# Reordering neighbouring steps in the four hand-written engine orders of a decoder-layer kernel

## What is computed

```
S = S * exp(g_t);  kv = k_t S;  delta = (v_t - kv) * beta_t
S = S + k_t^T delta;  o_t = q_t S
```

## Time and profile before

| what | value |
|---|---|
| median of 3 runs | 2258.28 us (2253.6 to 2272.47) |
| the profiled execution's own time | 2256.81 us |
| its span, first to last instruction | 2255.0 us |
| mean granted TensorE clock | 0.972 of full speed |
| TensorE matmuls busy | 2098.6 us (93% of the span) |
| TensorE weight loads busy | 1805.4 us (80%) |
| VectorE busy | 1646.6 us (73%) |
| ScalarE busy | 1385.5 us (61%) |
| GpSimd busy | 803.3 us (36%) |
| the chain that ended last | TensorE 83%, VectorE 10%, issue 3% |
| instruction transfers (two queues) | 264 packets, 4.33 MB, and 107 packets, 0.88 MB |

### The profile page before, as it was taken

How to read it: one execution, slowest core, us unless ns; L and a number is a source line. 1 busy time by engine, 2 the same in 40 slices (tenths; PEclk the granted TensorE clock), 3 DMA queues, 4 the chain that set the end, 5 groups by cost and what they waited for, 6 DMA issues and landing times.

```text
span 2255.0 us, 81282 instructions
## 1 busy us (share of the span) xinstructions
PE 2098.6 (93%) x33098; PEld 1805.4 (80%) x33130; DVE 1646.6 (73%) x5291; ACT 1385.5 (61%) x4262; POOL 803.3 (36%) x1845
## 2 busy tenths in 40 slices
PE   4899999999999999999999999999999999999975
PEld 3788888888788888888888888888888888888864
DVE  4577777777777777777777777777777777777743
ACT  3576556776555776555677655677655677555642
POOL 3333334433234333334333333343334343324321
PEclk8899999999999999999999999999999999999987
DMA  6000000000000000000000000000000000000000
GB/s 227 7 2 8 10 10 9 10 4 7 10 10 10 10 5 9 8 10 10 9 5 10 8 10 10 9 10 4 8 10 10 9 10 4 7 10 10 7 4 5
DMA packets 25795, 30.66 MB, mean 14 GB/s; under 512 B 9264, under 2 KB 22592, under 8 KB 24656
## 3 DMA queue, kind: packets, MB, share of 16 engines
q1 hardware_dynamic: 25424, 25.46, 3.5%
HBM read 21.25 MB, written 4.19 MB: 11 GB/s over the span
## 4 chain that ended last, share of the span: by engine, by line
PE 83%; DVE 10%; issue 3%; SPq 2%; ACT 1%; POOL 0%; DMA 0%; DVEq 0%; POOLq 0%
PE bank_b L644 11%; PE bank_a L464 10%; PE bank_b L746 5%; PE bank_b L652 5%; PE bank_a L474 5%; PE bank_b L769 5%; PE bank_b L605 5%; PE bank_a L536 3%; PE bank_a L546 3%; PE bank_b L700 2%; PE bank_a L582 2%; PE bank_a L589 2%; PE bank_a L512 2%; DVE smax L1169 2%; PE bank_b L677 2%
## 5 line engine op out<-in xcount | busy, mean ns | idle before, releaser
L1021 DVE SCALAR_TENSOR_TENSOR acc<-ypad,convw,acc 128x128 f32<-128x128 f32 x1536 | 426.7, 346 | 109.4 <-ACT acc L823 109.4
L464 PE MATMUL bank_a<-xnT,wqkvz 128*128 128x128 f32 x2048 | 251.1, 279 | 27.2 <-DVE scoreT L1092 24.6
L464 PEld LDWEIGHTS bank_a<-xnT,wqkvz 128*128 128x128 f32 x2048 | 243.0, 195 | 36.6 <-issue 34.9
L1433 POOL TENSOR_SCALAR lnv<-mv 128x1 f32<-128x1 f32 x128 | 24.8, 193 | 582.9 <-DVE mv L1111 580.2
L934 ACT ACTIVATE prob<-bank_b,nmax 128x128 f32<-128x128 f32 x512 | 181.4, 382 | 6.7 <-DVE nmax L1171 4.2
L1387 POOL TENSOR_TENSOR ostat<-ostat 128x4 f32<-128x4 f32 x64 | 18.7, 293 | 456.3 <-ACT gseg L888 456.2
L914 ACT ACTIVATE prob<-bank_b 128x512 f32<-128x512 f32 x64 | 38.2, 597 | 211.7 <-PE bank_b L644 211.7
L1076 DVE TENSOR_TENSOR ablk<-bank_a,const 128x128 f32<-128x128 f32 x256 | 72.6, 284 | 105.7 <-PE bank_a L536 102.7
L823 ACT ACTIVATE acc<-bank_a,convw 128x128 f32<-128x128 f32 x512 | 147.9, 397 | 0.0
L644 PE MATMUL bank_b<-x2T,wg 128*128 128x128 f32 x1024 | 141.7, 296 | 0.0
L546 PE MATMUL bank_a<-ablk,xblk 32*32 32x32 f32 x8192 | 123.3, 195 | 15.6 <-DMA bk<-in_bk_dram 9.2
(11 more groups left out here) (252 smaller groups left out, 5626.0 us busy)
## 6 DMA issues: line engine op xcount, KB each, us to landing
xin<-in_x_dram SPq DMA_DIRECT2D x32, 128.0 KB, 2.4
cin<-in_ctx_dram SPq DMA_DIRECT2D x32, 128.0 KB, 2.8
out_dram<-yout SPq DMA_DIRECT2D x32, 128.0 KB, 1.7
wqkvz<-in_wqkvz_dram SPq DMA_DIRECT2D x6, 512.0 KB, 6.6
wout<-in_wout_dram SPq DMA_DIRECT2D x1, 1024.0 KB, 9.6
wg<-in_wg_dram SPq DMA_DIRECT2D x1, 1024.0 KB, 11.3
wu<-in_wu_dram SPq DMA_DIRECT2D x1, 1024.0 KB, 13.1
wd<-in_wd_dram SPq DMA_DIRECT2D x1, 1024.0 KB, 14.9
```

Source lines behind the costliest of these rows:

```text
L464: last = mm(A[bank][:, b * P:(b + 1) * P], wqkvz[:, c, o:o + P], xnT[:, c, :], start=(c == 0), stop=(c == KC - 1))
L1021: stt(acc[:, c, :], ypad[:, c, k:k + P], convw[:, c, k:k + 1], acc[:, c, :], ALU.mult, ALU.add).then_inc(conv.sem, 1)
```

## The change

Only the four lists in `ORDER` change. Every step stays, with its instructions and waits as they were. Most moves are by one to four places. Some cross the end of a trip, so that a step changes its suffix with its place: TensorE's and DVE's `a_la11` goes from the start of a trip to the end of the one before, DVE's `a_u0` from the end of a trip to the start of the next, and on POOL `c_ln3` and `a_rq` go to the end of the trip before, `a_xr` from the last place of a trip to the second place of the next, and `b_mask` from the end of a trip to the middle of the next.

```diff
--- before.py
+++ after.py
@@ -110,23 +110,23 @@
 
 
 ORDER = dict(
-    pe="a_lb10@1 a_la11@1 b_gu0@2 b_gu1@2 a_lb11@1 a_la20@1 b_gu2@2 b_gu3@2 b_dn0@2 a_la21@1 a_lb20@1 a_xT "
-       "b_dn1@2 b_k@2 a_qk@1 a_lb21@1 a_la30@1 a_ba a_la31@1 a_lb30@1 a_lb31@1 b_y1T@2 a_pa@1 b_q@2 a_pb@1 "
-       "c_s a_mt@1 a_vT1@1 a_qkv0 a_sz0@1 c_pT1 a_sz1@1 c_pT2 c_pT0 a_o0@1 a_qkv1 c_pT3 a_o1@1 c_R a_z1 c_pv "
-       "a_z0 c_xo a_qkv2 a_qkv3 c_y2T a_ss c_h a_st c_c0 c_lg a_dec0 c_c1 c_wT a_kk c_spread a_dec1 c_pj0 "
-       "b_oT0 b_oT1 c_pj1 b_w0 b_w1 a_la00 b_cT a_la01 a_lb00 a_vT0 b_v b_x2T a_lb01 a_la10 b_router".split(),
-    act="b_sum@2 b_cT@2 b_x2T@2 b_rl@2 b_sg0@2 b_rt@2 a_sum b_sg1@2 a_xT a_ba a_mix3@1 b_y1T@2 a_zf@1 b_q@2 "
-       "a_zo@1 c_exp0 a_mt@1 c_exp1 c_exp2 a_sz0@1 a_qkv0 a_sz1@1 c_exp3 a_o0@1 a_qkv1 a_o1@1 c_pT1 c_pT0 "
-       "c_R a_ln a_mix0 a_z1 a_mix1 a_z0 a_sq a_qkv2 c_y2T a_st c_h a_qkv3 c_lt c_c0 a_seg c_te c_wT c_c1 "
+    pe="a_lb10@1 b_gu0@2 b_gu1@2 a_lb11@1 a_la20@1 b_gu2@2 b_gu3@2 b_dn0@2 a_lb20@1 a_la21@1 a_xT b_dn1@2 "
+       "a_qk@1 a_lb21@1 a_la30@1 b_k@2 a_ba a_la31@1 a_lb30@1 a_lb31@1 b_y1T@2 a_pa@1 b_q@2 a_pb@1 c_s "
+       "a_mt@1 a_vT1@1 a_qkv0 a_sz0@1 a_sz1@1 c_pT0 a_o0@1 c_pT1 a_qkv1 c_pT2 a_o1@1 c_pT3 a_z1 c_R c_pv "
+       "a_z0 c_xo a_qkv2 a_qkv3 c_y2T a_ss c_h a_st c_c0 c_lg c_c1 a_dec0 c_wT a_kk c_spread a_dec1 c_pj0 "
+       "b_oT0 b_oT1 c_pj1 b_w0 b_w1 a_la00 a_la01 b_cT a_lb00 a_lb01 a_vT0 b_v b_x2T a_la10 a_la11 b_router".split(),
+    act="b_sum@2 b_cT@2 b_x2T@2 b_rl@2 a_sum b_rt@2 b_sg0@2 a_mix3@1 b_sg1@2 a_xT b_y1T@2 a_zf@1 b_q@2 a_ba "
+       "a_zo@1 c_exp0 a_mt@1 c_exp1 c_exp2 a_sz0@1 a_qkv0 c_exp3 a_sz1@1 a_o0@1 a_qkv1 a_o1@1 c_pT1 c_pT0 "
+       "c_R a_ln a_mix0 a_z1 a_mix1 a_z0 a_sq a_qkv2 c_y2T a_st c_h a_qkv3 c_lt a_seg c_c0 c_te c_wT c_c1 "
        "a_dec0 a_dec1 b_oT0 b_oT1 a_mix2".split(),
-    dve="a_la11@1 a_lb10@1 a_la20@1 a_lb11@1 b_act0@2 a_xn a_conv32@1 b_act1@2 b_ys0@2 a_la21@1 a_lb20@1 "
-       "b_ys1@2 a_lb21@1 a_la30@1 a_la31@1 b_y1@2 a_lb30@1 a_lb31@1 a_pa@1 b_k@2 a_score@1 c_max0 c_max1 "
-       "a_low@1 c_max2 a_u1@1 c_max3 a_conv00 c_pT0 a_conv01 a_conv02 c_rec c_pT1 a_conv10 a_conv11 "
-       "a_core0@1 a_conv12 c_ao a_core1@1 c_sum2 c_y2 a_conv20 a_conv21 a_ss c_lb a_conv22 c_route a_conv30 "
-       "c_gc0 c_weight c_gc1 c_y4@3 a_lower a_init c_sum3 b_hid a_la00 c_y3 b_x2 a_la01 a_lb00 b_v a_la10 "
-       "a_lb01 a_u0 b_top a_conv31".split(),
-    pool="b_rd@2 c_ln3@3 b_rt@2 a_x b_ln0@2 a_ga a_rq@1 b_y1b@2 a_osc0@1 a_osc1@1 a_g c_ln1 c_rx c_sig c_y2b "
-       "a_sc c_ln2 b_rs b_mask b_xh a_xr".split(),
+    dve="a_lb10@1 a_u0@1 a_conv32@1 b_act0@2 a_lb11@1 a_la20@1 b_act1@2 a_xn b_ys0@2 a_la21@1 a_lb20@1 "
+       "b_ys1@2 a_lb21@1 a_la30@1 a_la31@1 b_y1@2 a_lb30@1 a_lb31@1 b_k@2 a_pa@1 a_score@1 c_max0 c_max1 "
+       "a_low@1 c_max2 a_u1@1 c_max3 a_conv00 a_conv01 c_pT0 a_conv02 c_rec a_conv10 c_pT1 a_conv11 "
+       "a_core0@1 c_ao a_core1@1 a_conv12 c_sum2 c_y2 a_conv20 a_ss a_conv21 c_lb a_conv22 c_route c_y4@3 "
+       "a_conv30 c_gc0 c_weight c_gc1 a_lower a_init c_sum3 b_hid a_la00 a_la01 c_y3 b_x2 a_lb00 a_lb01 "
+       "a_la10 a_conv31 b_v a_la11 b_top".split(),
+    pool="b_rd@2 a_xr@1 a_x b_rt@2 b_ln0@2 b_mask@2 a_ga b_y1b@2 a_osc0@1 a_osc1@1 c_ln1 a_g c_rx c_sig c_y2b "
+       "a_sc c_ln2 b_rs c_ln3 a_rq b_xh".split(),
 )
```

## The result

The changed kernel takes **2242.26 us** (median of 8 runs, 2236.21 to 2244.80), the kernel before 2260.04 (median of 8 runs beside and ahead of it, 2253.6 to 2272.47). The ratio is 0.9918 with a 95% interval of 0.990 to 0.9937: 0.8% faster, a gain of about 18 us. I had forecast 2262 us, a small loss. The profiled execution after took 2237.27 us by itself (span 2235.4), 19.5 us less than the one before. All medians of this document are of runs that agree with each other within 1.5%; one single run, of `pt_early` at 2624.91 us, stands far apart and is left out.

A forecast was written before the change was run, and what follows sets the result against it. It took TensorE, its matmuls busy 93% of the span, as the bound. Terms +5.4 - 0.9 - 2.2 + 1.9 = +4.2 us gave 2261.0 on the profiled execution, median 1.5 higher: 2262 us, range 2237 to 2284.

The forecast's parts named there:

- The wait for `a_low`: TensorE's a_qkv0 waits 0.8 us each for VectorE's a_low; the wait stays, cost 0, between -0.1 and +0.1 us a trip.
- `a_ba` ahead of the exp: On ACT, a_ba between b_q and a_zo delays exp and c_pv by 0.18 us a trip, +5.4 us; bounds 0 and 0.3.
- The end of a trip: VectorE's a_la01 ahead of b_x2, TensorE's a_lb01 earlier: gain 0.03 us a trip, about -0.9 us; bounds -0.1 and +0.2.
- rival B: New instruction stops in TensorE's unbroken run of a_la00 to a_lb01; slower, 2289 or 2292 us; chance 11%.
- The transfer of x: POOL's a_xr later, so x lands later for ACT; 1.1 us in hand, cost 0, at the longest landing 0.2 a trip.
- The mask: POOL's b_mask between b_ln0 and a_ga ends about when VectorE's b_k would start; 0 to 0.06 us a trip, taken 0.
- rival D: POOL's mask slowed in its new place, holding b_k, a_pa and a_zo; 0.4 us a trip, 2274 us; chance 3%.
- The instruction blocks: TensorE's stop at instruction 461 only moves into a_lb10, no change; the stops in a_pa go, -2.2 us.
- rival A: TensorE's stops and slow clock go: 2237 us, or 2212 to 2226 with a steady wait closing too; chance 14%.
- The second trip: a_xr falls behind POOL's packing of weights, so a_xT comes at about 61.5 instead of 59.61: +1.9 us once.

The follow-up runs named there:

- pt_early: x2_early with ACT's copies c_pT1 and c_pT0 moved ahead of its a_o1; 2233.35 us, ratio 0.9878 to the kernel before.
- low_early: Changed kernel's TensorE and VectorE lists, ACT's and POOL's of before, with VectorE's a_low moved ahead of c_max1; 2231.39 us.
- aba_back: The changed kernel with ACT's a_ba put back behind a_xT, where ACT is idle; 2232.49 us.
- x2_early: Changed kernel's TensorE and VectorE lists, old ACT and POOL lists, VectorE's b_x2 ahead of c_y3, c_y3's product in its own tile, c_y3, b_v, a_conv31 moved; 2217.88 us.
- pool_back: The changed kernel with POOL's list of the kernel before; 2244.27 us.
- lb01_alone: The kernel before with only a_la01 and a_lb01 moved, on TensorE and VectorE, to where the changed kernel has them; 2248.86 us.
- bk_alone: The kernel before with only b_k moved: on TensorE from behind b_dn1 to behind a_la30, on VectorE ahead of a_pa; 2245.89 us.
- bk_back: The changed kernel with b_k put back: on TensorE behind b_dn1, on VectorE behind a_pa; 2247.08 us.
- lb01_back: The changed kernel with a_la01, b_cT and a_lb01 put back to their old places, a_la11 left at the trip's end; 2289.04 us.
- after_idle: The changed kernel with VectorE's a_conv31 ahead of a_la10, so TensorE waits at each turn of a trip; 2296.64 us.

## Why the prediction was wrong, point by point

**The wait for `a_low`, cost 0.** Right (24.6 to 26.0 us). I had called it one that stays; low_early closed most of it with one move, and the time didn't move, so it isn't a reserve either.

**`a_ba` ahead of the exp, +0.18 us a trip (5.4 us).** Right in mechanism and place, too small: aba_back gave 0.3 us a trip (undisturbed, 66.59 to 66.27) and 10 us. The table load came 0.31 later, not 0.18: I had credited the step with idle time of ACT ahead of `a_zo`, and there was next to none. 0.3, my upper bound, was the value.

**The end of a trip, -0.03 us a trip.** Of the wrong sign, but inside my bounds. With `a_lb01` alone, `c_pv` to `b_gu0` takes 30.44 us instead of 30.14 (medians without disturbed trips); with `a_la11` 30.20, in the changed kernel 30.27. So +0.13 us a trip, about 4 us in all, where I took -0.9. The unbroken run of `a_la00` to `a_lb01`, where rival B saw a new stop, has none: 264 instructions there pass unharmed, as the next transfer begins ahead of the block (part 3). `b_x2T`'s wait was 0.3 us a trip that I had listed only as one that stays; x2_early shows it was the one worth closing.

**The transfer of x, 0.** Right. SP issues it right behind `a_xr`, and `b_sg1` ends 1.2 us ahead of `b_act1`'s start. SP, ACT's `a_sum` and its `b_sg1`, and the landing of x after, answering to the earlier trace rows:

```profile
977.51 0.33 SPq L402 DMA_DIRECT2D xin<-in_x_dram  x1
...
979.63 0.42 ACT L811 ACTIVATE junk_a<-xin 128x256 f32<-128x256 f32 x1 [4.89 <-DMA xin<-in_x_dram]
...
981.38 0.60 ACT L914 ACTIVATE prob<-bank_b 128x512 f32<-128x512 f32 x1 [0.15 <-PE bank_b L644]
...
DMA to landing us min/median/max: 1.9/2.1/3.8
```

**The mask, 0 to 0.06.** Too small for its stretch, and without effect on the whole. POOL's mask does hold `b_k` on VectorE: over 0.15 us in 11 trips of the changed kernel (2.8 us together, 1.2 of them in one) and in 26 of aba_back (5.3 us). Its two operations take 602 to 767 ns in the new place, 597 to 636 before. The kernel that differs in POOL's list alone, pool_back, takes 20.11 us from `b_gu0` to `c_s`, the changed kernel 20.34. But from `c_pv` to `b_gu0` pool_back takes 30.55 and the changed kernel 30.27, and their times are 2 us apart. So the mechanism of rival D is there, at half its price, and another move in the same list pays for it; which one, no run shows. The trip that I looked at:

```profile
993.20 1.12 DVE L1161 SCALAR_TENSOR_TENSOR kT<-bank_b,bk,madj 128x128 f32<-128x128 f32 x4 [0.17 <-POOL fill_bf L1406]
```

**The instruction blocks: this step failed.** I wrote that "the stop in `a_la11` comes at instruction 461. In the new order this is inside `a_lb10`, reached at the same time: no change". The count was right, and the block ahead of the boundary passes almost as fast (4.1 us for 3.8). What I had taken as fixed is when the next block's transfer begins: 1.0 to 1.3 us behind the entry instead of 2.9 to 3.5, now that the entry is in `a_lb01` and not at `a_vT0`. My rows held one stop and a count of transfers, and no start of a transfer beside an entry. The trip in which the same boundary brought no stop, at 846 us of the old trace, would have shown it. Term by term: 0 for the long stops, measured -10 us in `a_la` and -4.6 in `b_gu1`; the first went with lb01_alone's edit alone, which left 1.8 us of the second. -2.2 for `a_pa`, measured -1.0: one stop of 1.2 us is left, and I had written that none would be. That `b_k`'s place is what acts there, bk_alone and bk_back bear out (five stops to one, one to four). On the page of the Trainium skill that I had cited (Runtime: NRT & Kernel Launch, Instruction fetch mechanics), crossing a block is "mostly hidden". The traces bear on it with 18 stops of 16.2 us before and 4 of 2.8 us after: it holds for nearly all of the 264 blocks, and fails where a late transfer meets a short block. What I had set against rival A, that the count up to the boundary is the same, was true and decided nothing.

**The clock was tied to the stops, and is not.** In rival A I had priced it at 1.65 us for each long stop and nothing else. The runs show drops without a long stop (9 in lb01_alone, 18 in lb01_back, 21 in after_idle), and all drops together are worth 13 of the 31 us that came back. The Trainium skill (TensorE: Matmul & The Clock Gate, Terms) puts the loss at about the throttled time x (1 - K/N), with K/N the granted share of the clock, so x 0.5 at the half clock; the fits of the kernels with nine drops or more give 0.32 to 0.43 us for each us, 0.38 in the kernel before. By 0.5 the clock's part would be 17 us, not 13.

**The second trip, +1.9 us.** Right in place and slightly small: `a_xT` came at 62.09 instead of 59.61, +2.5. I had said 61.5.

```profile
62.09 0.69 PE L451 MATMUL bank_a<-const,xn 128*128 128x128 f32 x2 [3.07 <-DVE xn L1009]
```

In sum: the terms other than stops and clock came to +6.4 us in my working and to about +14 in the traces (12 in the trips, 2.5 once). The 0.42 us of a trip are 0.22 ahead of `c_pv` (`a_ba`), 0.13 at the turn and the rest between `b_gu0` and `c_s`. Rival A, to which I gave 14% for 25 us of stops and slow clock, gave about 31. I had rejected it with a count of instructions alone. The measured time lies inside my range, at its lower end, only because I had drawn the range out towards rival A: the path that I called the likely one would have ended 20 us higher. (One small slip in the working: the lower bounds of the terms, 0.18 and 0.07 a trip, come to 7.5 us in 30 trips, not 9. Nothing hangs on it.)

## What to carry to other kernels

Price an order by its undisturbed trip and by its disturbances apart: this change lost 12 us on the first and won 31 on the second, and with ACT's list left alone it would have won 28 us instead of 18. A stop for instructions is judged by three times, all in the trace: entry of the block, start of the next transfer, end of the block. A wait is a reserve only if the steps behind it are ready: of the three steady ones here, the reordering that closed the shortest (`b_x2T`, 0.3 us) paid 16 us, and those that shortened the two longer ones paid nothing or cost 15.

## What was not expected of the hardware

Waits of 0.6 to 1.0 us a trip, added among 32x32 matmuls, let the clock fall 18 to 23 times in 30 trips instead of once, and that costs some 30 to 50 us beyond the waits (0.40 to 0.43 us by the fits, for each of 75 to 116 us at 1.2 GHz). The start of an instruction transfer goes by the place of the block, from 1.9 us ahead of its entry to 5.6 us behind it, and at the boundary that brought the long stops it has two modes, 0.6 to 1.5 and 2.8 to 3.5 us behind the entry. What chooses between them, why POOL's list alone brought 13 drops instead of 10, and what starts the drops with nothing idle ahead, stays open.
